# Decoder megakernel: the entry of the last dense expert pass set between the sorted tiles instead of behind them

## The reference

```python
for _ in range(LOOPS):
    z_norm = _rmsnorm(z, norm_w)
    logits = z_norm @ router_w
    scores = jax.nn.softmax(logits, axis=-1)
    topk_vals, topk_idx = jax.lax.top_k(scores, TOP_K)
    topk_vals = topk_vals / (jnp.sum(topk_vals, axis=-1, keepdims=True) + EPS)
    cw = jnp.sum(jax.nn.one_hot(topk_idx, E, dtype=z.dtype) * topk_vals[..., None], axis=-2)
    ...
    for e in range(E):
        mixed = mixed + flat_cw[:, e:e + 1] * _swiglu(flat_z, w1[e], w3[e], w2[e])
    z = z + mixed.reshape(B, S, D)
```

## Time and profile before

| what | value |
|---|---|
| time of the kernel before, median of 3 runs | 584.07 us (582.03, 584.07, 587.35) |
| span of the profiled execution, first to last instruction | 578.4 us |
| the profiled execution's own device time | not listed; the runs listed are 3.6 to 9.0 us longer than its span |
| TensorE busy in that span | 492.7 us, 85% |
| VectorE / ScalarE / GpSimd busy | 444.4 / 278.8 / 202.7 us |
| mean granted clock of TensorE | 0.941 of full speed |

### The profile page before, as it was taken

The page is one execution under the profiler, slowest core; times in us unless marked ns, Lnnn a source line. Parts: engine busy times, 40 slices in busy tenths (PEclk is TensorE's granted clock), DMA queues, the critical chain, the costliest instruction groups (busy, mean ns, idle before and its releaser), DMA issues.

```text
span 578.4 us, 9279 instructions
## 1 busy us (share of the span) xinstructions
PE 492.7 (85%) x3133; PEld 284.3 (49%) x3133; DVE 444.4 (77%) x1174; ACT 278.8 (48%) x519; POOL 202.7 (35%) x169
## 2 busy tenths in 40 slices
PE   7799899999998989698998835655579999999866
PEld 5344566666665666465554401222224666666423
DVE  7589867666677357156775889999998789998996
ACT  4631356555443234253433347555530477776555
POOL 8624000000004104332500019899992245543030
PEclk9899999999999999898899965888789999998989
DMA  5500260000010201412200000000001000000001
GB/s 138 161 18 1 82 174 2 2 1 2 1 47 23 83 10 60 118 51 58 63 0 0 2 1 0 0 1 0 1 0 42 5 2 1 3 2 2 1 1 37
DMA packets 25250, 17.28 MB, mean 30 GB/s; under 512 B 2962, under 2 KB 24020, under 8 KB 25204
## 3 DMA queue, kind: packets, MB, share of 16 engines
q1 hardware_dynamic: 24180, 14.59, 8.8%
q0 software_dynamic: 1024, 2.10, 1.2%
HBM read 10.00 MB, written 5.51 MB: 27 GB/s over the span
## 4 chain that ended last, share of the span: by engine, by line
PE 31%; DVE 23%; issue 6%; POOL 6%; ACT 3%; DMA 1%; SPq 0%; DVEq 0%; POOLq 0%; ACTq 0%
PE PS L1331 7%; PE PS L806 5%; DVE PS L2184 5%; DVE VA L2197 4%; PE PS L1373 3%; PE PS L851 3%; PE PS L868 3%; DVE PS L2190 2%; POOL E L2142 2%; POOL OT L2600 1%; POOL sorted L2590 1%; POOL KSA L2134 1%; PE PS L2044 1%; PE PS L826 1%; DMA answers<-OT 1%
## 5 line engine op out<-in xcount | busy, mean ns | idle before, releaser
L851 PE MATMUL PS<-QM,KP 32*128 32x256 f32 x512 | 92.3, 400 | 1.2 <-ACT E L1039 0.8
L806 PE MATMUL PS<-KP,QP 32*128 32x256 f32 x512 | 78.0, 400 | 0.5 <-ACT QP L1017 0.5
L1039 ACT ACTIVATE E<-PS 128x512 f32<-128x512 f32 x100 | 56.2, 595 | 36.4 <-PE PS L851 24.3
L2590 POOL DMA_INDIRECT sorted<-VA,slot_of x16 | 15.7, 980 | 144.1 <-DVE expert_at L1723 127.0
L851 PEld LDWEIGHTS PS<-QM,KP 32*128 32x128 f32 x512 | 60.7, 184 | 6.2 <-issue 4.8
L1331 PE MATMUL PS<-XNT,KSA 128*128 128x512 f32 x128 | 62.0, 621 | 0.8 <-ACT XNT L1511 0.8
L356 PE MATMUL PS<-KSA,select 128*128 128x512 bf16 x64 | 25.6, 492 | 42.0 <-ACT KSA L2081 30.2
L806 PEld LDWEIGHTS PS<-KP,QP 32*128 32x128 f32 x512 | 51.3, 184 | 14.5 <-issue 10.1
L1114 DVE CUSTOM_DVE_ANT_0 SCR<-PS,KSA 128x256 f32<-128x256 f32 x128 | 47.5, 420 | 9.1 <-PE PS L806 8.3
L1109 DVE TENSOR_REDUCE MXT<-PS 128x2 f32<-128x512 f32 x64 | 41.0, 685 | 14.4 <-PE PS L806 14.4
L2565 POOL TENSOR_TENSOR VA<-VA,KSA 128x512 f32<-128x512 f32 x28 | 35.2, 1276 | 37.7 <-ACT VA L1044 37.7
(11 more groups left out here) (335 smaller groups left out, 1064.3 us busy)
## 6 DMA issues: line engine op xcount, KB each, us to landing
KSA<-in_w SPq DMA_DIRECT2D x2, 1024.0 KB, 7.0
sorted<-zeros SPq DMA_DIRECT2D x2, 960.0 KB, 6.4
answers<-OT SPq DMA_DIRECT2D x14, 128.0 KB, 1.8
KSA<-in_w SPq DMA_DIRECT2D x2, 512.0 KB, 9.7
QP<-sorted SPq DMA_DIRECT2D x4, 256.0 KB, 3.2
QP<-sorted SPq DMA_DIRECT2D x2, 448.0 KB, 5.2
X<-in_x SPq DMA_DIRECT2D x2, 256.0 KB, 3.5
SCR<-in_ctxT SPq DMA_DIRECT2D x1, 512.0 KB, 5.5
```

Of the source, the lines that this page charges most:

```text
L806: ins = pe.matmul(score_bank(n, i)[:, q * S:(q + 1) * S], QP[rows(i), g, t:t + P], KP[rows(i), g, b * S:(b + 1) * S], start=True, stop=Tru ...
L851: ins = pe.matmul(o[:, kt * S:(kt + 1) * S], KP[rows(i), g, t:t + P], QM[rows(i), g, b * S:(b + 1) * S], start=True, stop=True, skip_group ...
L1039: act.activation(slot(m, j), drain_bank(L, m, j), ACT.Exp).then_inc(sig("exps"), 1)
```

## The change

The mix of pass 1's answers moves from tiles 26 and 27 to tiles 22 and 23, the sums from tile 28 to 24, the norm from behind tile 29 to behind tile 26, and the turn and the copy to `XNT` into turn 28 of the tile loop on TensorE and ScalarE. On TensorE `unit_up(pe, 16)` stands right behind the tile loop, ahead of the transposes and down-products of the last tiles, and the router's products stand ahead of the very last tile's down-product. `unit_up(16)` writes bank 5, where the sorted rows were turned, and gets a wait for the last `take_sorted`. Nothing is added or left out in the computation.

```diff
-        SORTED_MIX_AT = 27
+        SORTED_MIX_AT = 23
+        LAST_STATS_AT, LAST_NORM_AT, LAST_TURN_AT = 24, 26, 28
...
             if g == UPS:
                 pe.wait_ge(sig("gated"), tile_step(TILES - 3))
+                pe.wait_ge(sig("sorted_taken"), 8)
...
+                if i == LAST_TURN_AT:
+                    pass_turn(pe, 3)
...
+            unit_up(pe, UPS)
             turn_tile(TILES - 2)
             tile_down(TILES - 3, starts[SLOT_TILES - 3])
             turn_tile(TILES - 1)
             tile_down(TILES - 2, starts[SLOT_TILES - 2])
+            pass_logits(pe, 3)
             tile_down(TILES - 1, starts[SLOT_TILES - 1])
-            pass_turn(pe, 3)
-            unit_up(pe, UPS)
-            pass_logits(pe, 3)
             unit_up(pe, UPS + 1)
             unit_up(pe, UPS + 2)
...
+                if i == LAST_TURN_AT:
+                    pass_scalar(act, 3)
             take_hidden(TILES - 2)
             take_hidden(TILES - 1)
-            pass_scalar(act, 3)
...
-                if i == 28:
+                if i == LAST_STATS_AT:
                     pass_stats(dve, ch, 3)
-            pass_norm(dve, ch, 3)
+                if i == LAST_NORM_AT:
+                    pass_norm(dve, ch, 3)
             take_answers(2 * PAIRS - 2)
             take_answers(2 * PAIRS - 1)
```

## The result

The changed kernel took 575.22 us in the median of 4 runs (574.99 to 577.28), the kernel before 583.05 in 4 runs of the same comparison (581.88 to 587.35; the fourth run is new). The ratio is 0.9867, interval [0.9818, 0.9917]: 7.8 us, 1.3%, faster. 579.0 was forecast, range 576.0 to 582.6: right in sign, too small in size, and the time lies 0.8 us under the range. The means further down take in every execution, also the slow ones, those more than 1.5% above the fastest of their kernel: 19 of 90 of before and none of the changed kernel's ten, and without them a gain of 7.0 us becomes 6.2 (0.8).

The account below looks back on a forecast made before the run. TensorE's own products were taken to bound the kernel on both sides of the seam, where 7.1 us were not full-clock work. Waits 3.4 plus clock 1.7 gave 5.1 us: 584.07 - 5.1 = 579.0 us, range 576.0 to 582.6.

Parts of the forecast that it names:

- The waits: TensorE's waiting at the seam between sorted tiles and pass 3: 3.5 us, of which 0.1 stays, so 3.4 saved.
- that case: If unit 16 and the router's products failed to cover the last tiles' handshakes, 1.3 us stay and the waits give 2.2.
- A misread row: Profile page, TensorE's row: clock digits said to fall to 6, 5 in slices 19 and 20, one dent at the seam.
- The entry's timing: VectorE's norm, moved earlier, was to end at 262.8, 0.6 us ahead of TensorE's need at the turn, 263.45.
- gathers there in time: Gathered rows, needed by the mix at 254.26, were to land by about 253, over 1 us early; wait taken as 0.
- the new `take_sorted` wait: Unit 16's added wait for the last copy of sorted rows was to cost 0, that copy being done some tiles before.
- First down-product: Sign in the new profile: pass 3's first down-product at about 275.0 in place of 281.97, at clock 1.00 throughout.
- The clock term: Slow clock at the seam, 3.56 us lost in the profile; 1.7 us gain taken for the median run, ends 0 and 3.56.
- rival 2: At the seam every run before paid the whole clock fall: gain 7.0 us, time 577.1; chance 0.2.
- The fall of 0.76 over 236 to 243: Another clock fall, 3.4 us at the low level, 1.7 lost; its size was taken for the seam's clock term.
- The level: Starting time from which the gain was taken: the median of three runs of the kernel before, 584.07 us.
- Rivals 3 and 4: 3: gain given back behind the seam, 582 to 584 us, chance 0.13. 4: mix at tile 22 waits for rows, slower, 0.05.

Follow-up runs that it names:

- turn_27: The changed kernel with the entry's turn and copy one tile earlier on TensorE and ScalarE (27 in place of 28); one execution took 576.64 us.
- filled waits: The kernel before with extra unread products in TensorE's two waits at the seam; cut behind the experts, 5 and 3 products: mean 333.4 us against 337.5 without.
- cut kernel: A kernel without the scan, the second cross-attention and the last feed-forward; mean 337.5 us for the kernel before, 329.3 for the changed one.
- cut_before_2: Second call of the kernel before without scan, second cross-attention and last feed-forward, otherwise unedited; mean 337.5 us over the 12 runs of both calls.
- model seams: Imitations of the seam, 36 per kernel, appended to the kernel before cut behind the experts; over 48 double-wait draws 1.6 us lost per seam.
- before_warm: The kernel before, whole, with 10 and 6 extra unread products in TensorE's two waits at the seam; median 584.81 us over 12 runs.
- before_again: The kernel before, unedited, run again for more spans and clocks; median 584.58 us over 12 runs, its profiled execution 575.95 us.

## Why the prediction was too small

**The waits**: right. 3.4 us forecast; 3.25 between the two traces in which the clock stays up, 3.3 by the rest over 90 and 10 executions. Two small errors nearly cancel in it, which is luck: with the clock up the stretch holds 15.15 - 11.43 = 3.7 us that are not work, not 3.5 (the fall costs 3.37, not 3.56), and 11.90 - 11.43 = 0.5 is left where 0.1 was allowed. Of the gain the early entry alone brings 2.6 (15.15 - 12.11 - 0.44; 2.2 was forecast for that case), the new order of TensorE's products 0.66.

**A misread row**: "its clock digits fall to 6, 5 in slices 19 and 20 (260 to 289 us)" is wrong. Counted out, slices 19 and 20 of the earlier trace rows both have 8, and the 6 and 5 are slices 24 and 25, 333 to 361 us, in the scan. The fall at the seam was read from the earlier trace rows, and no term of the sum used the digits.

**The entry's timing**: right. Norm 0.6 ahead of the turn (forecast 0.6), gathers there in time, no wait of the mix, the new `take_sorted` wait free, the second mix still behind its gather. `turn_27` shows the margin from the other side. First down-product at 278.31, not 275.0, only because the trace runs 3 us late from before the seam.

**The clock term**: mis-sized, and this is the step that failed. I put 1.7 us on "so for the median run the ends are 0 and 3.56, and I take 1.7", by the length of a fall at another place. At the seam itself the traces show 3.37 us lost in five of six, 2.8 (0.6) in the mean; the time at the low level gives 3.7 (1.1) between the whole kernels, and the filled waits in the cut kernel 4.1 (1.3). The last two have draws at other places in them and can't all be the seam's, since one fall there costs 3.37; the traces are the firmer source. Each of the three lies about twice its error above 1.7. With their 2.8 and the waits' 3.25 the gain would be 6.1, against 7.0 (0.8) measured. The fall does come and go, as I wrote, but it was in five of six traces and then whole; a median over such runs contains it. So rival 2 (the whole fall in the typical run, 577.1) was nearest, though its wording, every run, is refuted by one trace. The Trainium skill, page "TensorE: Matmul & The Clock Gate", section "What's actually happening", has the number of slow matmuls at a kernel's start vary between runs of one kernel. The traces show the same kind of variation at this seam, with 0 us at the low level in one and 6.8 in five. The fall of 0.76 over 236 to 243 was a poor neighbour: it stands at another hole, and its length is a draw too (10.2 us at the low level in three other traces). The nearest row was the one at the seam itself.

**The level**: 1.0 us of the miss. 584.07 was a median of three runs; the fourth moved it to 583.05, and 90 executions give 583.08. And the four runs of the changed kernel lie 0.9 under the mean of ten, 576.07, with which the forecast's miss would be 2.9 us, 1.0 by the level and 1.9 by the gain, and the time would lie at the edge of the range, 576.0: that it fell outside is in part the luck of four runs. The forecast took the spread of three runs, 5.3 us, as a sign of the fall alone; the cut kernels that ran 12 times show spreads of 7 to 14 us, of which a fall at the seam can give 3.4; `cut_before_2`, for one, fell twice more near 188 and 198 us.

**What stays open.** The model seams lose 1.6 us each, the real one 2.8 or more. What the model lacks is not known (GpSimd and the DMAs are at work at the real seam, and its handshakes are not the same), and six draws are few. What the fall costs in the mean is not settled: 2.8 by the traces, 3.7 (1.1) by the listed clocks, and `before_warm` shows no gain at all from filled waits in the whole kernel. Rivals 3 and 4 did not happen.

## What to carry to other kernels

A wait on TensorE costs its length and, with some chance, half of the slow stretch behind it; price that chance from the wait itself, seen in several executions, and when the one trace at hand shows the fall, count it whole until another trace shows otherwise. Compare two kernels by the mean of many executions and split the time with the listed clock into slow clock and rest: the mean of the rest over a dozen executions repeats to a few tenths and shows a gain of 3 us that single times hide. Where a trace can be had, read the stretch itself in several: here it repeats to 0.01 us apart from the fall. When a step is to be set between others in a fixed order, add up the busy time of the engine that carries it from its first possible start; here that gave the place of the norm to 0.1 us.

## What the runs showed of the hardware

- Equal waits at the same place of the program were followed by products at 2.4 GHz in one trace (`before_again`) and at 1.2 GHz for 6.8 us in five others: stretches of 15.15 and 18.5 us. In `before_again` TensorE had been busy for 1.29 of the 3 us from 268 to 271, in `before` for 0.99, with the same pair of waits in it, moved by 0.4 us.
- A single wait of 1.1 us behind three handshakes brought the clock down 1 time in 12; two waits of 1.1 and 0.7 us with four transposes between them 33 times in 48.
- Products that nobody reads, in the waits, kept the clock up there in 4 of 4 traces; with 5 and 3 of them the stretch was 15.15 us, where it was 18.5 with a fall.
- Falls inside a span last 3.4 us or multiples of it in these traces: 6.8 and 10.2, 20.5 once near the start of `before_warm`, 23.9 and 27.3 in the scan.
- What lies around the span is the same, 1.7 to 1.8 us, for all whole kernels. A profiled execution with a span of 578.4 was one of about 580.1 us, well under its kernel's median.
